# One joint order for the first two iterations of a two-block attention kernel, and identity products on TensorE ahead of it

## The chip, the cores and the metric

The kernel runs on one core of a Trainium2 chip. The metric is the device time of one execution in microseconds (us). All times come from three runs of the kernel before and one profiled execution of it.

## The reference, cut to what matters

Two residual attention blocks for 16 batch items `b`, all in float32. `x` is `(16, 256, 512)`.

```python
# block 0: 8 heads of 32, over 512 tokens, query = key = value
q = x^T @ Wq^T                       # per head qh
logits = (scale*qh@qh^T * cmask + (1-cmask)*-1e30) * rmask
x = x + (softmax(logits) @ qh @ Wo^T)^T
# block 1: 16 heads of 32, over 256 rows of width 512
xn = rms_norm(x, g_norm) * (1 + scale_b) + shift_b      # scale_b, shift_b = cond[b] @ W_emb + b_emb
q, k, v = split(xn @ W_qkv);  q, k = rms_norm(q, g_q), rms_norm(k, g_k)
o = softmax(q@k^T / sqrt(32)) @ v
x = x + o + o @ W_out
```

## The kernel before, in words

Work is written out by hand for each engine, and every engine follows its own list in order; semaphores join them. `pipeline(steady, special)` runs steps `i = -1 .. 17`. In step `i` block 0 of item `i` (stages A: heads 0 to 3, B: heads 4 to 7), block 1 of item `i-1` (stage C) and the output product of item `i-2` are interleaved. Steps 2 to 14 use one list, `iteration`; steps -1, 0, 15, 16 and 17 have lists of their own, and so the first two batch items meet only as far as those lists let them.

The steps, by the names used below:
- `project0` (L396): query projection, two float32 products of 128x512 into PX. ACT takes it (`take_query`, L1059), POOL masks it (`mask_query`, L1903), ACT rounds it to QHI and DVE makes the rest QLO (`split0`).
- `maxima0` (L411) and the DVE reduction L1539: row maxima of the raw scores, four key blocks for each of the two head groups. `rows0` (L426) transposes them; ACT sends them to row 96 of B0 with a DMA (L1079).
- `stack0`: six SP DMAs for each head, which put QHI and QLO under each other into A0 and B0. `score0` (L442) multiplies these; ACT takes the exponential (L1040) into a buffer of E. There are two score banks, PS0 and PS1.
- `values_weighted0` (L469), `weights_summed0` (L480; it needs the sums that `add_keys0` makes on POOL, L1916, and on DVE, L1557), `take_sums0` and `invert0` (DVE, L1577), `scale0`, `context0`, `out0` (L508), `residual0`, `squares`, `rstd`, `norm`, `norm_rows` (L519), `modulate`: from the probabilities of block 0 to XNT, the input of block 1.
- `qk` (L530), `take_heads`, `square_heads`, `square_sums`, `add_eps`, `power_heads` (POOL, L1928), `norm_heads` (POOL, L1935), `heads_rows` (L548), `round_heads`, `split1`, `maxima1` (L420, DVE L1546), `rows1` (L430), `stack1` (six SP DMAs for each of four), `values1`, `score1` (L456), `values_and_sums1` (L491, L494), `out1` (L564).
- `modulation` (L372): eight groups of four products of 128x128 by 128x16; a float32 product is two instructions on TensorE, so these are 64. They use WEMB, which before lies in E. ACT issues all weight loads (L1484 to L1492) before its first activation.

The order in which shared PSUM banks (PX, the four banks of PM, PO) pass from one user to the next is written in the tables BIG, MAXES and CONTEXT_TAKEN; `big`, `small` and `quad_free` turn them into waits. An instruction of TensorE that waits holds all that stands behind it in its list.

Of the kernel before, what the change touches and what calls it, by code (L numbers as in the profile page):

```python
# [7 lines left out]
F32 = mybir.dt.float32  # L8
F32R = mybir.dt.float32r
ALU = mybir.AluOpType  # L10
# [29 lines left out]
class Order:  # L40
# [4 lines left out]
    def __init__(self, *uses, special=None):  # L45
        self.uses, self.special = uses, special or {}

    def of(self, i):
        return self.special.get(i, self.uses)

    def find(self, key, i):
        return [k for k, _, _ in self.of(i)].index(key)

    def count(self, i, stop, place):
        return sum(0 <= i + off < NB and place in (None, where) for _, off, where in self.of(i)[:stop])

    def upto(self, key, i, place=None):

        if i < -1:
            return 0  # L60
        return sum(self.count(j, None, place) for j in range(-1, i)) + self.count(i, self.find(key, i) + 1, place)

    def ahead(self, key, i, place=None):

        return self.upto(key, i, place) - (place in (None, self.place(key)))

    def total(self, place):
        return sum(self.count(j, None, place) for j in range(-1, NB + 2))

    def place(self, key):  # L70
        return next(where for k, _, where in self.uses if k == key)
# [11 lines left out]
            (("C", 3), -2, 0), (("C", 0), -1, 0), (("C", 1), -1, 0), (("C", 2), -1, 0), ("A", 0, 0), ("B", 0, 0)),  # L83
        16: (
            ("A", 0, 0), ("B", 0, 0), (("C", 3), -2, 0), (("C", 0), -1, 0), (("C", 1), -1, 0), (("C", 2), -1, 0)),
# [32 lines left out]
            (("p1", 0), -1, 0), (("p1", 1), -1, 0), (("p1", 2), -1, 0), (("p1", 3), -1, 0), (("w1", 0), -2, 0),  # L118
            (("w1", 1), -2, 0), (("v1", 0), -1, 0), (("v1", 1), -1, 0), (("p0", 0), 1, 0), (("p0", 1), 1, 0),
            (("w0", 0), 0, 0)),  # L120
# [5 lines left out]
            (("p0", 0), 1, 0), (("p0", 1), 1, 0), (("w0", 0), 0, 0), (("p1", 0), -1, 0), (("p1", 1), -1, 0),  # L126
# [2068 lines left out]
```

## Time and profile before

| | us |
|---|---|
| median of 3 runs | 1313.63 |
| lowest, highest | 1311.67, 1318.56 |
| the profiled execution, its own time | 1316.98 |
| its span in the profile | 1315.2 |
| TensorE busy in the span | 1247.5 (95%) |
| VectorE, ScalarE, GpSimd busy | 1034.5, 767.3, 773.4 |
| mean granted TensorE clock, share of 2.4 GHz | 0.969 |

The span is what the engines show between first and last instruction; the time has 1.8 us more around it. TensorE is the busy engine, but its share is a mean over a long even middle and two ends that look different, so the views to read are those by stretch and the instructions in order of time at both ends.

### The profile page before, as it was taken

The numbers are of one execution on the slowest core, as the hardware profiler recorded it, in microseconds if no ns is written. First come the engines' busy times: TensorE is split into PE (matmuls) and PEld (weight loads), VectorE is DVE, ScalarE is ACT, GpSimd is POOL, SyncE is SP. The second block draws the span as 40 slices with busy tenths as digits, with TensorE's granted clock in tenths as the row PEclk, the third lists the DMA queues.
The fourth block names the chain that finished last, engine by engine and source line by source line (L and its number), as shares of the span: only waits on it lengthen the run. The fifth ranks groups of instructions, "written<-read, shape, count | busy, mean of one in ns | idle before, by whom it ended". The sixth has DMA issues, their size and how long they took to land.

```text
span 1315.2 us, 20714 instructions
## 1 busy us (share of the span) xinstructions
PE 1247.5 (95%) x6768; PEld 581.5 (44%) x6768; DVE 1034.5 (79%) x916; ACT 767.3 (58%) x1393; POOL 773.4 (59%) x391
## 2 busy tenths in 40 slices
PE   6979899999999999999999999999999999998877
PEld 4424354544444454444445454444545444443433
DVE  4665778878887887889787888888788888877654
ACT  1525566665656666565657666566666656564514
POOL 0245658476665838575574847566583766647442
PEclk8769899999999999999999999999999999999998
DMA  8322544437253433636354342735444363632332
GB/s 279 98 52 78 113 105 99 108 84 169 82 142 101 112 98 92 150 81 162 94 117 111 91 119 81 170 89 124 110 102 107 91 161 82 147 77 57 83 68 61
DMA packets 77960, 143.01 MB, mean 109 GB/s; under 512 B 21536, under 2 KB 23072, under 8 KB 77856
## 3 DMA queue, kind: packets, MB, share of 16 engines
q1 hardware_dynamic: 69136, 126.17, 39.1%
q10 hardware_dynamic: 8720, 15.51, 3.9%
q8 instruction: 58, 0.95, 0.3%
q14 instruction: 46, 0.38, 0.1%
HBM read 32.02 MB, written 8.39 MB: 31 GB/s over the span
## 4 chain that ended last, share of the span: by engine, by line
PE 80%; POOL 6%; issue 4%; DVE 3%; ACT 3%; SPq 2%; ACTq 1%; DMA 1%; POOLq 0%; DVEq 0%
PE PX L530 25%; PE PS L442 9%; PE PO L469 8%; PE PX L564 7%; PE PS L456 6%; PE PO L491 5%; POOL RQK L1928 5%; PE PM L411 4%; PE PX L508 2%; PE PM L508 2%; PE PO L494 2%; PE PM L420 2%; SPq L2071 1%; PE PM L480 1%; PE PM L548 1%
## 5 line engine op out<-in xcount | busy, mean ns | idle before, releaser
L1040 ACT ACTIVATE E<-PS,KBIAS 128x512 f32<-128x512 f32 x512 | 340.0, 686 | 199.0 <-PE PS L442 151.3
L530 PE MATMUL PX<-WQKV,XNT 128*128 128x512 f32 x768 | 383.9, 603 | 3.1 <-ACT V L1018 1.6
L1539 DVE TENSOR_REDUCE NM<-PM 128x4 f32<-128x2048 f32 x128 | 292.1, 2282 | 79.4 <-PE PM L411 79.4
L1916 POOL TENSOR_TENSOR E<-E 128x1024 f32<-128x1024 f32 x112 | 263.1, 2368 | 120.8 <-PE PO L469 107.6
L442 PE MATMUL PS<-B,A 97*128 97x512 f32 x512 | 288.1, 600 | 6.2 <-ACT E L1040 5.3
L1946 POOL TENSOR_TENSOR KQLO<-E 128x1024 f32<-128x1024 f32 x64 | 151.5, 2368 | 229.3 <-ACT E L1047 227.6
L1928 POOL TENSOR_TENSOR RQK<-RQK,HALF 128x16 f32<-128x16 f32 x64 | 211.1, 3303 | 96.6 <-DVE RQK L1627 96.6
L1047 ACT ACTIVATE E<-PS 128x512 f32<-128x512 f32 x256 | 146.9, 597 | 111.1 <-PE PS L456 110.9
L530 PEld LDWEIGHTS PX<-WQKV,XNT 128*128 128x128 f32 x768 | 136.5, 190 | 103.7 <-issue 89.1
L1546 DVE TENSOR_REDUCE NM<-PM 128x8 f32<-128x2048 f32 x64 | 146.4, 2288 | 37.5 <-PE PM L420 37.4
L442 PEld LDWEIGHTS PS<-B,A 97*128 97x128 f32 x512 | 93.3, 192 | 161.6 <-issue 110.2
L456 PE MATMUL PS<-B,A 97*128 97x256 f32 x512 | 136.6, 373 | 4.7 <-ACT E L1047 2.5
L469 PE MATMUL PO<-E,V 128*32 128x512 f32 x1024 | 139.4, 628 | 0.0
L564 PE MATMUL PX<-WOUT,OT 128*128 128x512 f32 x248 | 125.5, 600 | 0.9 <-ACT QK L1018 0.9
L1646 DVE RECIPROCAL T<-T 128x256 f32<-128x256 f32 x64 | 111.5, 1742 | 15.8 <-ACT T L1018 15.8
L456 PEld LDWEIGHTS PS<-B,A 97*128 97x128 f32 x512 | 81.3, 191 | 82.9 <-issue 64.3
L1557 DVE TENSOR_TENSOR E<-E 128x1024 f32<-128x1024 f32 x80 | 99.0, 1238 | 23.5 <-ACT E L1040 16.1
L1577 DVE RECIPROCAL R<-R 128x256 f32<-128x256 f32 x64 | 109.9, 1736 | 1.1
L1018 ACT ACTIVATE QK<-PX 128x512 f32<-128x512 f32 x64 | 38.2, 597 | 86.6 <-PE PX L530 86.6
L396 PE MATMUL PX<-XB,WQ 128*128 128x512 f32 x128 | 66.5, 645 | 10.5 <-DMA XB<-x 5.8
L411 PE MATMUL PM<-QHI 32*128 32x512 f32 x512 | 67.3, 514 | 8.5 <-DVE NM L1539 5.2
L1620 DVE TENSOR_REDUCE SSQ<-YSQ 128x16 f32<-128x512 f32 x64 | 43.7, 682 | 38.8 <-ACT YSQ L1103 37.6
(80 smaller groups left out, 1354.3 us busy)
## 6 DMA issues: line engine op xcount, KB each, us to landing
A<-QHI SPq DMA_DIRECT2D x256, 64.0 KB, 2.0
B<-QHI SPq DMA_DIRECT2D x256, 64.0 KB, 2.0
A<-KQHI SPq DMA_DIRECT2D x128, 128.0 KB, 2.4
B<-KQHI SPq DMA_DIRECT2D x128, 128.0 KB, 2.4
XB<-x SPq DMA_DIRECT2D x16, 512.0 KB, 4.0
A<-QLO SPq DMA_DIRECT2D x128, 64.0 KB, 2.0
B<-QLO SPq DMA_DIRECT2D x128, 64.0 KB, 2.0
X<-x ACTq DMA_DIRECT2D x16, 512.0 KB, 4.9
```

The lines of the kernel that those rows point to most:

```text
L442: mm(PS[n % 2][:, :], A0[0:97, h, g * P:(g + 1) * P], B0[0:97, h, :], start=True, stop=True).then_inc(score_full, 1)
L456: last = mm(PS[n % 2][:, kb * N1:(kb + 1) * N1], A1[0:97, hq, c, kb * P:(kb + 1) * P], B1[0:97, hq, c, :], start=True, stop=True)
L469: last = mm(PO[h * DH:(h + 1) * DH, :], V0[:, q, g, h * DH:(h + 1) * DH], E[:, probs(seg, i, g), h, :], start=(g == 0), stop=(g == KB0 - 1))
L530: last = mm(PX[:, :], XNT[:, c, t * P:(t + 1) * P], WQKV[:, c, part * DM:(part + 1) * DM], start=(c == 0), stop=(c == 3))
L564: last = mm(bank, OT[:, c, t * P:(t + 1) * P], WOUT[:, c, :], start=(c == 0), stop=(c == 3))
L1040: fn(E[:, probs(seg, i, g), h, :], PS[n % 2][:, :], ACT.Exp, bias=KBIAS[:, g, b:b + 1], scale=SCALE).then_inc(exp_done, 1)
L1047: fn(E[:, probs("C", i, c), h, :], PS[n % 2][:, :], ACT.Exp, scale=SCALE_RAW).then_inc(exp_done, 1)
L1539: v.tensor_reduce(NM0[:, q, :].rearrange("p (h k) -> p h k", k=KB0)[:, :, kb], PM[:, :, :], axis=AX.X, op=ALU.max, negate=True).then_inc(m ...
L1546: v.tensor_reduce(NM1[:, :].rearrange("p (h c a) -> p h c a", c=Q1, a=2)[:, :, c, :], PM[:, :, :].rearrange("p h (a k) -> p h a k", a=2), ...
L1916: g_.tensor_tensor(running(seg, i)[:, heads_, :], running(seg, i)[:, heads_, :], E[:, probs(seg, i, g), heads_, :], ALU.add).then_inc(done, 1)
L1928: g_.tensor_tensor(rqk, rqk, HALF[:, :], ALU.pow).then_inc(rqk_done.sem, 1)
L1946: g_.tensor_tensor(key_sums(c), e[:, :, 0:N1], e[:, :, N1:2 * N1], ALU.add).then_inc(esum_done.sem, 1)
```

## The change

It touches the first three and the last three lists, not `iteration`.

1. Steps 0 and 1 get one joint list, `iterations_0_and_1`, on every engine; step 1 is then empty. The tables get matching entries, and `Order` counts them with a dictionary instead of by walking.
2. `keep_warm(n)`: n products of the identity with itself into PS1, which nobody reads. The calls in the diff are 14, 4, 8, 8, 12, 8 and 16, 70 in all.
3. WEMB has its own place (over B1), is loaded by SP directly behind XB; WO, WQKV and WOUT are loaded by SP in `load_weights`, behind a wait for `row0_in[1]`. ACT issues only CT, BEMB, GN and GQK, at once.
4. ACT issues half of the first item's `stack0`.
5. `modulation` runs as two blocks of four groups, around the last `maxima0` of the first head group.
6. Step 15 gets another order (on POOL `masked_out` goes from the place behind the first `add_keys0` to the place behind the last `norm_heads`). In step 16 `qk` alternates between PX and a bank of PM, `norm_heads` is on DVE, `values_and_sums1` of item 14 goes behind the four `qk`, the rows of maxima go out in two halves (`rows1_half`, four DMAs each), and ACT issues one `stack1` of four. Step 17 has its `out1` in another order.

```diff
+            def keep_warm(n):
+                pe.wait_ge(ident_set.sem, 3)
+                for _ in range(n):
+                    mm(PS[1][:, 0:P], IDENT[:, :], IDENT[:, :], start=True, stop=True)
...
             def iteration_before(i):
+                keep_warm(14)
                 project0(i, i + 1, 0)
                 project0(i, i + 1, 1)
+                keep_warm(4)
                 maxima0(i, i + 1, 0, 0)
+                keep_warm(8)
                 maxima0(i, i + 1, 0, 1)
-                modulation(0)
-                modulation(1)
-                modulation(2)
+                keep_warm(8)
                 maxima0(i, i + 1, 0, 2)
-                modulation(3)
-                modulation(4)
-                modulation(5)
+                modulation(0, 1, 2, 3)
                 maxima0(i, i + 1, 0, 3)
-                modulation(6)
-                modulation(7)
+                modulation(4, 5, 6, 7)
                 rows0(i, i + 1, 0)
-
-            def iteration_0(i):
+                keep_warm(12)
+
+            def iterations_0_and_1(i):
+                maxima0(i, i, 1, 0)
+                keep_warm(8)
+                project0(i, i + 1, 0)
+                keep_warm(16)
+                score0("A", i, i, 0, 0, 0)
                 values0(i, i, 0)
...
                 score0("B", i, i, 1, 3, 0)
+                maxima0(i, i + 1, 0, 1)
+                project0(i, i + 1, 1)
+                maxima0(i, i + 1, 0, 2)
+                values_weighted0("B", i, 1, 1)
                 score0("B", i, i, 1, 3, 1)
...
                 weights_summed0("B", i, 1)
...
+                score0("A", i + 1, i + 1, 0, 0, 0)
+                values0(i + 1, i + 1, 0)
+                values0(i + 1, i + 1, 1)
+                score0("A", i + 1, i + 1, 0, 0, 1)
+                score0("A", i + 1, i + 1, 0, 0, 2)
+                score0("A", i + 1, i + 1, 0, 0, 3)
                 out0(i, i, 0)
                 out0(i, i, 1)
...
+                norm_rows(i, i)
+                score0("A", i + 1, i + 1, 0, 1, 2)
+                score0("A", i + 1, i + 1, 0, 1, 3)
+                qk(i + 1, 0, 0, 1, 2, 3)
...
             def iteration_16(i):
                 qk(i, 0, 0, 1, 2, 3)
-                values_and_sums1(i - 1, i - 2, 3)
                 qk(i, 1, 0, 1, 2, 3)
                 qk(i, 2, 0, 1, 2, 3)
                 qk(i, 3, 0, 1, 2, 3)
-                out1(i, i - 2, 0, 0, 1)
+                out1(i, i - 2, 0, 0)
+                values_and_sums1(i - 1, i - 2, 3)
...
+        def heads_bank(b, k):
+            return PM[:, 3, :] if b == NB - 1 and k % 2 else PX[:, :]
...
+            def load_weights():
+                sp.wait_ge(row0_in[1].sem, row0_in[1].at(0))
+                sp.dma_start(WO[:, :, :], wo_t.rearrange("(c p) n -> p c n", p=P)).then_inc(wo_in.sem, 16)
+                sp.dma_start(WQKV[:, :, :], w_qkv.rearrange("(c p) n -> p c n", p=P)).then_inc(wqkv_in.sem, 16)
+                sp.dma_start(WOUT[:, :, :], w_out.rearrange("(c p) n -> p c n", p=P)).then_inc(wout_in.sem, 16)
...
+            def iterations_0_and_1(i):
+                load_mask(i)
                 stack0(i + 1, 0, 2)
                 stack0(i + 1, 0, 1)
                 stack0(i + 1, 0, 3)
+                load_weights()
+                stack0(i + 1, 0, 0)
```

## Rows read from the trace of the kernel before

**Rows 1.** Busy time by stretch: length, PE, PEld, DVE, ACT, POOL, clock, DMA, GB/s.

```profile
200.00:275.50 75.50, 74.56 (x427) 34.78 (x419) 63.41 (x57) 47.72 (x88) 48.30 (x25) 1.00 0.46 113
1163.90:1243.10 79.20, 71.59 (x395) 32.87 (x395) 56.73 (x52) 45.50 (x81) 44.33 (x23) 0.98 0.32 77
1243.10:1286.40 43.30, 34.61 (x136) 14.57 (x133) 23.19 (x24) 9.50 (x16) 18.23 (x9) 0.96 0.32 71
1286.40:1315.20 28.80, 24.14 (x150) 12.14 (x148) 13.11 (x10) 12.29 (x22) 9.45 (x4) 0.87 0.13 42
104.00:182.00 78.00, 72.35 (x381) 32.83 (x381) 55.49 (x48) 47.03 (x86) 46.31 (x24) 0.92 0.37 86
37.40:103.90 66.50, 51.34 (x187) 19.18 (x187) 43.73 (x44) 28.42 (x51) 24.11 (x12) 0.71 0.31 79
```

**Rows 2.** Stretches of 2 us, TensorE alone: length, busy, clock, DMA, GB/s.

```profile
16.00:18.00 2.00, 2.00 (x7) 1.00 1.01 415
...
24.00:26.00 2.00, 2.00 (x11) 0.50 1.06 288
...
52.00:54.00 2.00, 1.93 (x12) 1.00 0.44 109
```

**Rows 3.** In order of time, the opening: start, length, engine, line, work, idle before.

```profile
12.14 1.28 ACT L1059 ACT_TABLE_LOAD   x1 [12.14 <-issue]
...
14.26 3.50 PE L396 MATMUL PX<-XB,WQ 128*128 128x512 f32 x4 [4.72 <-ACT QF L1059]
...
18.32 2.29 DVE L1539 TENSOR_REDUCE NM<-PM 128x4 f32<-128x2048 f32 x1 [1.40 <-PE PM L411]
...
27.29 5.30 PE L372 MATMUL PO<-CT,E 128*128 128x16 f32 x24
...
37.39 0.60 ACTq L1079 DMA_DIRECT2D B<-NMT  x1
...
37.46 1.09 PE L403 MATMUL PM<-IDENT,QF 128*128 128x128 f32 x4 [0.40 <-issue]
...
40.01 1.22 PE L442 MATMUL PS<-B,A 97*128 97x512 f32 x2
...
101.55 1.06 PE L519 MATMUL PM<-IDENT,YSQ 128*128 128x128 f32 x8 [0.16 <-DVE YSQ L1605]
```

**Rows 4.** In order of time, where the stages of steps 0 and 1 begin.

```profile
59.45 0.99 PE L442 MATMUL PS<-B,A 97*128 97x512 f32 x2 [0.41 <-DMA B<-NMT]
...
90.98 3.78 PE L508 MATMUL PX<-XB,WO 128*128 128x512 f32 x4 [0.58 <-DVE XB L1588]
...
103.89 1.95 PE L530 MATMUL PX<-WQKV,XNT 128*128 128x512 f32 x2
...
159.07 0.80 PE L456 MATMUL PS<-B,A 97*128 97x256 f32 x2
...
181.92 1.02 PE L530 MATMUL PX<-WQKV,XNT 128*128 128x512 f32 x2
```

**Rows 5.** Groups of the page: busy, mean ns of one, idle before and releaser.

```profile
L1916 POOL TENSOR_TENSOR E<-E 128x1024 f32<-128x1024 f32 x112 | 263.1, 2368 | 120.8 <-PE PO L469 107.6
...
L1577 DVE RECIPROCAL R<-R 128x256 f32<-128x256 f32 x64 | 109.9, 1736 | 1.1
```

**Rows 6.** DMA issues of the first 60 us: KB each, us to landing.

```profile
WQKV<-w_qkv ACTq DMA_DIRECT2D x1, 3072.0 KB, 15.2
...
WOUT<-w_out ACTq DMA_DIRECT2D x1, 1024.0 KB, 19.3
```

**Rows 7.** In order of time, the waits of steps 15 and 16.

```profile
1186.92 0.62 POOL L1907 TENSOR_SCALAR CBI<-CBI 128x512 f32<-128x512 f32 x1 [7.63 <-DMA CBI<-cond]
...
1195.35 1.94 PE L480 MATMUL PM<-E,ONES 128*32 128x512 f32 x8 [4.03 <-DVE E L1557]
...
1256.91 3.70 PE L530 MATMUL PX<-WQKV,XNT 128*128 128x512 f32 x8 [0.69 <-ACT QK L1018]
...
1267.11 1.09 PE L548 MATMUL PM<-IDENT,QK 128*128 128x128 f32 x8 [1.23 <-POOL QK L1935]
```

More of the change, by code:

```diff
@@ L324, in cond_resid @@
         n1_full = ev("n1_full", 1)
+        n1_half = [sem(f"n1_half{j}") for j in range(2)]
+        row1_half_in = [sem(f"row1_half_in{j}") for j in range(2)]
         row1_in = ev("row1_in", 16)
@@ L382, in small, with modulation @@
                 return PM[:, k, :]
+            def modulation(*ns):
+                pe.wait_ge(mod_in.sem, 16 * 3)
+                pe.wait_ge(ct_in.sem, 16)
+                for n in ns:
+                    for c in range(4):
+                        last = mm(PO[:, n * NB:(n + 1) * NB], WEMB[:, c, n * P:(n + 1) * P], CT[:, c, :],
+                                  start=(c == 0), stop=(c == 3))
+                if ns[-1] == 7:
+                    last.then_inc(mod_full.sem, 1)
+            def keep_warm(n):
+                pe.wait_ge(ident_set.sem, 3)
+                for _ in range(n):
+                    mm(PS[1][:, 0:P], IDENT[:, :], IDENT[:, :], start=True, stop=True)
             def quad_free(key, i):
@@ new lines, in iterations_0_and_1 @@
+                score1(i + 1, i, 1, 2)
+                score1(i + 1, i, 1, 3)
+                maxima0(i + 1, i + 2, 0, 2)
+                score1(i + 1, i, 2, 0)
+                out0(i + 1, i + 1, 0)
+                score1(i + 1, i, 2, 1)
+                score1(i + 1, i, 2, 2)
+                out0(i + 1, i + 1, 1)
+                score1(i + 1, i, 2, 3)
+                maxima0(i + 1, i + 2, 0, 3)
+                values_and_sums1(i + 1, i, 0)
+                score1(i + 1, i, 3, 0)
+                values_and_sums1(i + 1, i, 1)
@@ L873, in iteration_15 @@
-                score0("A", i, i, 0, 2, 3)
                 qk(i, 2, 3)
@@ L1047, in exp1, with stack0, stack1 @@
                 fn(E[:, probs("C", i, c), h, :], PS[n % 2][:, :], ACT.Exp, scale=SCALE_RAW).then_inc(exp_done, 1)
+            def stack0(b, q, hq):
+                act.wait_ge(qlo_done.sem, qlo_done.at(b, q + 1))
+                act.wait_ge(score_full, SCORES.upto(("AB"[q], 15), b - 1))
+                for dst, src in stack0_rows(q, hq):
+                    act.dma_start(dst, src).then_inc(stack0_in[q][hq].sem, 16)
+            def stack1(i, b, hq):
+                for k in range(4):
+                    bank = MAXES.place(("tq", k))
+                    act.wait_ge(bank_taken[bank], MAXES.upto(("tq", k), i, bank))
+                act.wait_ge(score_full, SCORES.upto(("C", 15), b))
+                for dst, src in stack1_rows(hq):
+                    act.dma_start(dst, src).then_inc(stack1_in[hq].sem, 16)
             def take_context0(seg, i, b, q):
```

808 lines of the change are left out of this document (544 added, 264 removed), and 12 rows, old and new, of the table special.

## The prediction

> **What bounds the kernel now.** I read the busy times by stretch first, because the change touches only the ends. In the even middle one step takes 75.5 us, of which TensorE is busy 74.6 at full clock [rows 1]: it is the bound there, and `iteration` is not changed, so steps 2 to 14 should give and take nothing. The front is another matter. Steps 0 and 1 take 66.5 and 78.0 us; TensorE is busy 51.3 and 72.4 of these, at a granted clock of 0.71 and 0.92 [rows 1], so part of the busy time is half-speed work. The end takes 79.2, 43.3 and 28.8 us with 71.6, 34.6 and 24.1 busy. There a chain over several engines is the bound, and TensorE waits in its places. So I then read the instructions in order of time at both ends, and ask for each stage which wait ends last.
>
> **The clock in the front.** Full clock at 16 to 18 us, behind four dense projection instructions; 0.50 at 24 to 26 although TensorE is busy the whole time with `modulation`; full again at 52 to 54, behind another projection [rows 2, 3]. So the dense wide products were followed by a rise, the modulation's narrow ones were not.
>
> **What one identity product costs.** It is two instructions with a 128x128 weight and 128 moving columns. The nearest rows are the transposes of the same shape: four in 1.09 us at low clock, eight in 1.06 at full [rows 3]. Taking off one latency (about 0.4 and 0.25 us) leaves 0.22 and 0.11 us each, so a product costs 0.44 us at the low clock and 0.22 at the high one. The ends are 0.27 and 0.13 an instruction with the latency spread in. All 70 cost 15 us high or 31 low.
>
> **The opening, step by step.** I take TensorE's start at 4.0 us, an estimate: it needs the WQ load, and not XB as the first projection did. Fourteen products end near 9.7 if the clock rises about two thirds through. Projection 1.7, to 11.4. ACT was held by its own DMA issues to 12.1 and then loaded its table in 1.28 [rows 3]; now five small issues end near 3.5 us, but the table load may still stand behind the wait (0 or 1.28; I take 1.28, since it sat in front of the activation). So `take_query` comes near 12.7, where it came at 13.4. With the second projection at full clock (1.7 for 3.5 [rows 3]) the first reduction starts near 16.8 for 18.3, gain 1.5. Each of the next rounds is bound by the 2.29 us reduction plus 0.7; eight products (1.8 high, 3.5 low) fit under that only at full clock. Modulation is 64 instructions, at 0.22 each 14.1 us at low clock, 7.0 at high [rows 3]. Full clock throughout would bring `rows0` to 30.3, where it was 36.7. But the modulation blocks are just what ran in the low stretch, so I expect the fall near 27 and `rows0` near 33.8. Its data lands about 2.6 us after the issue, as it did from 37.39 to 40.01 [rows 3], so near 37. What holds the first score is then TensorE's own list: 36 products, one `maxima0` and a projection. Twelve products low 5.3, maxima 0.6, eight high 1.8, projection 1.8, sixteen high 3.5: the first score at 46, **6 us later than before**. This is the price of the products that lie on the path; the first 34 are nearly covered. Ends: 40.5 (never low) and 51 (fall at once and products low to the sixteenth).
>
> The page on the clock of the Trainium skill (TensorE: Matmul & The Clock Gate, "What's actually happening") says that the chip sets the clock by how busy TensorE has been lately. Taken as share of busy time, that rule would keep the modulation at full clock and give the first score at 40.5; the row of 24 to 26 us, 2.00 busy of 2.00 at 0.50, speaks against it.
>
> **Stage A of item 0** took 59.45 - 40.01 = 19.4 us [rows 3, 4], with half of it at low clock. Now one maxima round and a projection are already done, and the clock is high. What ends last is three reductions in a row with one add between (3 x 2.3 + 3 x 0.6 + 1.2), a row transpose, a copy and the row's DMA, from 2 us after the first score: 15.
>
> **From stage B to the first `qk`**, before 103.89 - 59.45 = 44.4 [rows 4]. POOL is the long lane: first add 4.5 after the start, four adds of 2.37 [rows 5], a mask 1.3, `scale0` 1.3, one more add: sums ready at 21. On DVE `take_sums0` 0.7, two reciprocals of 1.74 [rows 5], scale and context 1.4: `out0` could start at 27.4. The maxima of item 1 go through DVE before this, 4 x 2.3, and fit between. In TensorE's list, though, four scores of item 1 stand ahead of `out0`, and the first needs a `stack0` that SP issues behind `load_weights`. These 4.25 MB took 15 to 19 us to land among other traffic [rows 6]; at the about 410 GB/s that the opening moved [rows 2] they need 10.5. SP is at them near 13.5; I take it that the stack waits for what its own queue holds ahead (if not, it lands in time and 3 us go), so it lands near 26, `out0` starts near 28.6. From `out0` to `qk` it took 12.9 [rows 4], with the first product block at low clock; at high, and with one reduction squeezed in, 10.9. Sum 39.5, gain 5.
>
> The Trainium skill (DMA: Bandwidth & Descriptors, "Queues, rings and completion order") says that one engine's ring is consumed in order. That agrees with the choice made here; no row of before shows it, since there the stacks and the weights had different issuers.
>
> **From the first `qk` to that of step 2**, before 78.0 [rows 1, 4]. Clock 0.92 means 12.5 us at half speed, costing 6.2; I let 5.5 of it go, since nothing thins TensorE's list there now. Eight scores, two transposes, one weighted value and one maxima of stage A are done beforehand: 6. Left: 66.5. The chain of item 0's heads does not forbid it: four `power_heads` and norms on POOL, four maxima, rows and stacks give 44 to the first C score, where it was 159.07 - 103.89 = 55.2 [rows 4], and the C stage keeps its 22.9.
>
> Front: 46 + 15 + 39.5 + 66.5 = 167.0 against 181.9 [rows 4], **gain 14.9**.
>
> **Step 15.** POOL stood 7.63 us before `masked_out` on the mask's DMA, with `power_heads` and `add_keys0` behind it; for this DVE's add came late and TensorE idled 4.03 us and ran the next 3 at half speed [rows 7]. Moving `masked_out` behind the heads takes this away: 5.5 us. Of the 7.6 idle in the step [rows 1] no more than 8 can go. Next late is the `stack1` chain, so I take 5.
>
> **Step 16.** `qk` on one bank ran 3.70 and a 0.69 wait [rows 7], four times; two banks drop three gaps of 0.85, and `values_and_sums1` goes behind them: 3.5. Heads now meet DVE's norm, not a POOL queue; I count it equal. Three stacks on SP instead of four, and halves of the rows: the last stack is 3.85 earlier, the first C score needs only the first half. Together 7 of the 43.3 us [rows 1]. The C stage after that gets eight ACT issues of half a microsecond and keeps its 28.8.
>
> End: **gain 12**, between 5 and 17.
>
> **The sum.** 1316.98 - 14.9 - 12 = 1290.1 for an execution like the profiled one. Its time lay 3.35 over the median, so 1313.63 - 26.9 = 1286.7, say 1287.
>
> **The rivals.**
> 1. *Clock high through the modulation.* First score at 40.5 and shorter products: 1281. For it: the products before and between. Against: rows 2. Chance 0.2.
> 2. *The joint list stalls.* The stack behind the weights lands not at 26 but with the 19.3 of WOUT added to 15.5, at 35, and `out0`, the scores and all of step 1 wait 9 us; another 4 are lost where `project0` now stands behind a maxima round and ACT's list behind `take_query`. 1300. For it: rows 6. Against: those loads shared the rings with more traffic. Chance 0.2.
> 3. *The products don't lift the clock, and lie on the path.* As modulation did, they keep TensorE busy at 0.50. Place: ahead of the first score. Then 14 + 4 + 16 products, both modulation blocks (14.1) and 36 more products (15.8) all run low, the first score is at 64, 18 later than in my sum; stage A takes 19.4 (+4.4) and B some 5 more; and if it also costs the clock of `qk`, 3 more: 1287 + 30 = 1317, slower than before. It decides from a first score at about 64: below that the end's 12 us cover it. Against: the transposes at 101.55 ran at full clock [rows 3], and a projection has the same weight. Chance 0.1.
> 4. My own case, 1279 to 1295: 0.5.
>
> **How the numbers follow.** 0.5 + 0.2 + 0.2 + 0.1. The likeliest gives 1287. The range reaches down past rival 1 with the end's better bound (1281 - 5, and the stack early, 3), to 1272, and up past rival 2 with a poor end (1300 + 5), 1305; rival 3 is outside. A measurement of this kernel can tell about 0.5%, 6.6 us, from no change. Faster by more (under 1307): 0.87, all but rival 3 and a thin part of rival 2. Within: 0.08. Slower: 0.05.
>
> **What would show it.** Right: granted clock 1.00 in the rounds of `maxima0`, a drop in the modulation, the first score near 46; `qk` of step 2 near 167; steps 2 to 14 at 75.5 each; the end from there 139 long in steps 15 to 17. Wrong: a first score before 42 or after 55; a score of item 1 waiting on a stack DMA for more than 5 us; a steady step that changed; POOL idle at `masked_out` without use to TensorE.

## The result, and the profile after

| | before | after |
|---|---|---|
| median, us (9 runs each, in turn) | 1316.17 | 1308.59 |
| lowest to highest | 1311.67 to 1318.56 | 1307.71 to 1313.58 |
| profiled execution, its span | 1316.98, 1315.2 | 1308.48, 1306.2 |
| mean granted clock | 0.969 | 0.982 |

The ratio is 0.9957 (0.9941 to 0.9973): the change takes 7.6 us off, where 27 were forecast, and 1287 lies 21.6 below what came. The signs were right, the size was not, and the time lies outside the range.

The first view is the stage borders, read from the instructions in order of time as in [rows 3, 4]. "First score" is item 0's first, "B" its first score of the second head group; times are in the span.

| start of, us | before | forecast | after |
|---|---|---|---|
| first score | 40.0 | 46 | 43.65 |
| stage B | 59.45 | 61 | 59.1 |
| `out0` of item 0 | 91.0 | 89.6 | 95.4 |
| first `qk` | 103.9 | 100.5 | 108.1 |
| C of item 0, its first score | 159.1 | 144.5 | 161.2 |
| `qk` of step 2 | 181.9 | 167.0 | 183.0 |
| from there to the end of the span | 1133.3 | 1121 | 1123.2 |

So the end gave 10.1 of the 12 forecast, and the front gave nothing: it is 1.1 longer. The rest of this text asks where its 16 us are.

The view by stretches of the kernel after (length, PE, PEld, DVE, ACT, POOL busy, clock, DMA share, GB/s). The rows are, in turn: to the first score; stage A; B to `out0`; `out0` to the first `qk`; to the first C score; to `qk` of step 2; an even step; steps 15, 16; the C stage at the end.

```profile
3.90:43.60 39.70, 37.89 (x236) 32.68 (x237) 19.65 (x22) 3.63 (x8) 3.15 (x3) 0.87 0.64 175
43.60:59.10 15.50, 13.25 (x65) 5.29 (x63) 8.72 (x5) 11.02 (x20) 6.03 (x3) 0.89 0.00 1
59.10:95.40 36.30, 24.46 (x106) 9.40 (x106) 23.76 (x18) 16.53 (x29) 14.12 (x7) 0.82 0.57 181
95.40:108.10 12.70, 9.89 (x33) 4.16 (x32) 5.83 (x8) 6.22 (x14) 3.09 (x2) 0.77 0.15 39
108.10:161.20 53.10, 48.02 (x213) 19.43 (x213) 36.97 (x34) 27.45 (x49) 34.37 (x18) 0.95 0.43 101
161.20:183.00 21.80, 19.30 (x151) 11.24 (x147) 17.84 (x19) 13.84 (x29) 7.80 (x4) 1.00 0.40 103
...
200.00:275.50 75.50, 74.58 (x420) 34.86 (x419) 63.48 (x57) 47.88 (x87) 48.38 (x25) 1.00 0.42 104
...
1165.60:1237.70 72.10, 69.47 (x393) 31.94 (x391) 52.44 (x50) 44.91 (x79) 45.97 (x22) 1.00 0.35 85
1237.70:1274.60 36.90, 32.51 (x134) 14.00 (x130) 26.77 (x30) 9.88 (x17) 14.28 (x5) 0.94 0.35 82
1274.60:1306.20 31.60, 24.97 (x153) 12.75 (x153) 9.85 (x10) 12.55 (x23) 9.46 (x4) 0.90 0.12 40
```

The even step is that of [rows 1], 75.5 with 74.6 busy. In B to `out0` TensorE is busy for 24.5 of 36.3: no other row above has as much idle time. TensorE in order of time, after, shows what it is:

```profile
91.06 0.80 PE L500 MATMUL PS<-B,A 97*128 97x512 f32 x1 [6.96 <-DMA B<-QLO]
...
95.42 3.61 PE L569 MATMUL PX<-XB,WO 128*128 128x512 f32 x4
98.83 2.31 PE L569 MATMUL PM<-XB,WO 128*128 128x512 f32 x4
...
105.72 1.21 PE L580 MATMUL PM<-IDENT,YSQ 128*128 128x128 f32 x8 [2.48 <-DVE YSQ L1882]
```

The first score of item 1 waits 6.96 us on a DMA of its stack. The context for `out0` was ready at 88.9, but its products stand behind that score. The queue of SP (second number: us spent on the issues) tells why the stack is late:

```profile
62.62 0.51 SPq L2439 DMA_DIRECT2D A<-QHI  x1
...
74.78 0.58 SPq L2427 DMA_DIRECT2D WO<-wo_t  x1
75.41 0.50 SPq L2428 DMA_DIRECT2D WQKV<-w_qkv  x1
75.95 0.51 SPq L2429 DMA_DIRECT2D WOUT<-w_out  x1
76.56 0.51 SPq L2439 DMA_DIRECT2D A<-QHI  x1
...
79.65 0.59 SPq L2439 DMA_DIRECT2D B<-QLO  x1
```

Three other stacks are issued from 62.62 on, the weights behind them at 74.78, and this head's stack at 76.56 to 80.24. It lands near 91, 11 us after its last issue. Windows of 2 us (length, PE, PEld, DVE, ACT, POOL, clock, DMA share, GB/s) show the DMA engines full up to 88 and at 0.82 behind it, and the clock going down at the end of the wait:

```profile
80.00:82.00 2.00, 1.04 (x9) 0.24 (x9) 2.00 (x3) 0.63 (x2) 0.61 (x1) 1.00 1.00 421
...
84.00:86.00 2.00, 0.10 (x4) 0.00 (x0) 1.97 (x2) 1.11 (x2) 0.00 (x0) 1.00 1.00 383
...
88.00:90.00 2.00, 0.00 (x0) 0.00 (x0) 0.87 (x2) 0.00 (x0) 0.00 (x0) 0.86 0.82 238
```

So `out0` ran at the low clock (3.61 us for four instructions; 1.97 in e5 below). The first `qk` block did too, 6.27 us for eight, but behind another wait: the 2.48 us on DVE at 105.72. Between the two the clock was up again, since eight instructions took 1.06 us at 101.31.

### The profile page after: what moved, and what is told of

It is laid out like the page before. It is cut to its first block, busy times and chain, and to the rows that moved or that the text cites. A ratio compares the mean times of both kernels' runs of the same rounds, so it can differ in the third digit from the quotient of the medians.

```text
span 1306.2 us, 21009 instructions
## 1 busy us (share of the span) xinstructions
PE 1249.7 (96%) x6909; PEld 594.1 (45%) x6909; DVE 1030.0 (79%) x920; ACT 768.3 (59%) x1394; POOL 767.7 (59%) x387
## 4 chain that ended last, share of the span: by engine, by line
PE 74%; POOL 6%; DVE 6%; SPq 5%; issue 4%; ACT 2%; DMA 2%; ACTq 1%; DVEq 0%
PE PX L598 24%; PE PS L500 8%; PE PO L530 7%; PE PX L632 6%; PE PS L517 5%; POOL RQK L2266 5%; PE PO L552 5%; SPq L2447 4%; PE PM L463 4%; PE PX L569 2%; PE PM L569 2%; PE PO L555 2%; PE PM L472 2%; PE PM L580 1%; PE PS L434 1%
## 5 line engine op out<-in xcount | busy, mean ns | idle before, releaser
L598 PE MATMUL PX<-WQKV,XNT 128*128 128x512 f32 x752 | 377.6, 606 | 0.7 <-DVE XNT L1889 0.3
L2254 POOL TENSOR_TENSOR E<-E 128x1024 f32<-128x1024 f32 x112 | 262.9, 2366 | 118.0 <-PE PO L530 95.4
L500 PE MATMUL PS<-B,A 97*128 97x512 f32 x512 | 285.3, 593 | 12.7 <-DMA B<-QLO 7.0
L2266 POOL TENSOR_TENSOR RQK<-RQK,HALF 128x16 f32<-128x16 f32 x64 | 211.4, 3310 | 81.0 <-DVE RQK L1904 80.6
L598 PEld LDWEIGHTS PX<-WQKV,XNT 128*128 128x128 f32 x752 | 134.7, 192 | 101.0 <-issue 91.5
L530 PE MATMUL PO<-E,V 128*32 128x512 f32 x1024 | 134.5, 607 | 0.6 <-ACT E L1207 0.6
L517 PEld LDWEIGHTS PS<-B,A 97*128 97x128 f32 x512 | 81.6, 191 | 84.8 <-issue 67.7
L552 PE MATMUL PO<-E,V 128*32 128x256 f32 x1024 | 68.5, 385 | 0.3 <-ACT T L1185 0.3
```

The lines of the kernel that those rows point to most:

```text
L500: mm(PS[n % 2][:, :], A0[0:97, h, g * P:(g + 1) * P], B0[0:97, h, :], start=True, stop=True).then_inc(score_full, 1)
L517: last = mm(PS[n % 2][:, kb * N1:(kb + 1) * N1], A1[0:97, hq, c, kb * P:(kb + 1) * P], B1[0:97, hq, c, :], start=True, stop=True)
L530: last = mm(PO[h * DH:(h + 1) * DH, :], V0[:, q, g, h * DH:(h + 1) * DH], E[:, probs(seg, i, g), h, :], start=(g == 0), stop=(g == KB0 - 1))
L598: last = mm(bank, XNT[:, c, t * P:(t + 1) * P], WQKV[:, c, part * DM:(part + 1) * DM], start=(c == 0), stop=(c == 3))
L2254: g_.tensor_tensor(running(seg, i)[:, heads_, :], running(seg, i)[:, heads_, :], E[:, probs(seg, i, g), heads_, :], ALU.add).then_inc(done, 1)
L2266: g_.tensor_tensor(rqk, rqk, HALF[:, :], ALU.pow).then_inc(rqk_done.sem, 1)
```

## The experiments

Kernels of one table were timed in turns with the kernel before, whose medians were 1314.8, 1314.2, 1314.6, 1315.2 and 1313.6 in the five sets of runs (the last set is e17 and e18). "Base" is the kernel of e5, and of e9. Medians and ratios with intervals:

| run | us | ratio to before | first score | first `qk` | `qk` of step 2 |
|---|---|---|---|---|---|
| e1 stack ahead | 1305.4 | 0.9937 (0.992 to 0.9955) | 44.0 | 103.9 | 178.0 |
| e2 end only | 1307.9 | 0.9949 (0.9936 to 0.9962) | 39.9 | 103.8 | 181.8 |
| e3 no products | 1303.6 | 0.9925 (0.9909 to 0.994) | 38.5 | 105.3 | 179.4 |
| e4 34 early products | 1299.1 | 0.9891 (0.9874 to 0.9908) | 35.9 | 104.3 | 179.2 |
| e5 early, stack ahead | 1296.3 | 0.9865 (0.9846 to 0.9883) | 36.0 | 91.8 | 167.1 |
| e9 the same again | 1299.2 | 0.9867 (0.9843 to 0.9891) | 39.0 | 98.5 | 172.6 |
| e6 none, stack ahead | 1295.8 | 0.9861 (0.9849 to 0.9874) | 37.6 | 98.0 | 171.7 |
| e17 the same again | 1298.8 | 0.9881 (0.9858 to 0.9905) | 37.9 | 98.7 | 172.6 |
| e7 early, early weights | 1301.0 | 0.99 (0.9886 to 0.9914) | 39.5 | 100.2 | 175.5 |
| e8 early, separate lists | 1307.2 | 0.9953 (0.994 to 0.9966) | 38.4 | 101.8 | 179.2 |
| e10 short reciprocals | 1298.9 | 0.9868 (0.9845 to 0.9892) | 36.1 | 100.8 | 175.5 |
| e11 maxima first | 1298.2 | 0.9871 (0.9849 to 0.9894) | 36.1 | 96.1 | 173.7 |
| e12 half rows by SP | 1295.9 | 0.9862 (0.9836 to 0.9888) | 36.4 | 96.7 | 171.5 |
| e13 norm first | 1301.6 | 0.989 (0.9863 to 0.9917) | 39.0 | 99.3 | 174.4 |
| e14 short values | 1298.5 | 0.9869 (0.9852 to 0.9886) | 36.1 | 100.5 | 175.7 |
| e15 early mask | 1306.2 | 0.9923 (0.9906 to 0.9941) | 36.1 | 98.7 | 173.9 |
| e16 none, norm first | 1300.0 | 0.9884 (0.9864 to 0.9904) | 37.8 | 102.3 | 175.9 |
| e18 none, half rows by SP | 1300.7 | 0.9895 (0.9873 to 0.9918) | 37.6 | 98.4 | 173.8 |

The last three columns come from one profiled execution, the median from four to six; where both are read, note that e4's profile was its slowest execution (1304.2) and e5's its fastest (1292.2). Medians of different sets are compared below too. Where their intervals overlap, the difference is not shown, and the text says so.

### Two suspects: the stack's place and the late products

e1, the stack issued ahead of the weights:

```diff
-                load_weights()
                 stack0(i + 1, 0, 0)
+                load_weights()
```

> One line moved in SP's joint list: the stack of head 0 of item 1 is issued ahead of the three weight loads, not behind them. In the trace after, the first score of item 1 waited 6.96 us for that stack (it landed at 91, issued 76.6 to 80.2, behind 4.25 MB issued from 74.8), with the out0 products behind it although their input was ready at 88.9. Theory A (the stack waits in SP's own ring behind the weights, and TensorE's list hangs on it): the score goes near 84.5, out0 near 89.5 where it was 95.4, the whole run 5 to 7 us shorter than the changed kernel, near 1302. Theory B (the DVE chain to the context is what ends last anyway, or the DMA engines are the limit, so that the stack is as late): within 1 us of the changed kernel, 1308.

The wait on the stack is gone from the trace, `out0` starts at 91.5 for 95.4, and the median falls by 3.2. That is less than theory A had, and as the two intervals overlap it is not clear of the scatter. A wait of 2.6 us with no releaser named is left at the same score. The DMA view of 78 to 83 us (KB of each, us from issue to landing) tells what it is, first after, then e1:

```profile
B<-QLO SPq DMA_DIRECT2D x1, 64.0 KB, 11.4
B<-NMT ACTq DMA_DIRECT2D x1, 8.0 KB, 4.9
```

```profile
B<-QLO SPq DMA_DIRECT2D x1, 64.0 KB, 2.1
B<-NMT ACTq DMA_DIRECT2D x1, 8.0 KB, 5.1
```

The stack's transfers, ahead of the weights, land in 2 us for 11. The row of maxima that the same score needs, 8 KB on ACT's queue, still takes 5.1 us beside the weights; in the opening of before it took 1.8. It was issued at 81.99, so it landed at 87.1, and the score starts at 87.17. The same sum gives the start of that score within 0.2 us in e5, e6, e9 and e12, where the row took 4.9 to 6.3. So the weights hold this score in two ways, and the earlier stack takes away one.

e2 has the front of before and the end of after:

> Steps -1, 0 and 1 and the weight loads as in the kernel before, with no products; steps 15 to 17 as in the changed kernel. Theory A (the end carries all of the gain, the front gives nothing or takes a little, as the stage starts of the two traces say: the end 10.3 us shorter, the front 1.1 longer): 10 us under the kernel before, 1306, that is 1 to 3 under the changed kernel. Theory B (the end's gain depends on the state in which the front leaves the pipeline, or the front gives its part): 1310 or more.

It takes 7.0 us off the kernel before: no difference is shown to the 7.6 that the whole change gives.

e3 leaves all products out, e4 the 36 behind the last `rows0` of the opening:

```diff
-                keep_warm(12)
...
-                keep_warm(8)
                 project0(i, i + 1, 0)
-                keep_warm(16)
```

> The changed kernel without the 70 identity products, all else the same. Theory A (products on the path cost more than the clock gives: 36 of them stand ahead of the first score): the first score near 36 to 39, stage A at the low clock some 4 us longer, the end 2 to 4 us earlier, 1305. Theory B (they hold the clock up, and without them the opening runs at 1.2 GHz all through): first score no earlier than 40, stage A 19 us as before, stage B starts later than 59; 1312. Theory C (what decides the front is the stack behind the weights, and any gain ahead of it is swallowed there): 1308 within 1.

> The changed kernel with the first 34 products and without the 36 between the row transpose and the first score. Theory A: first score near 36, 7.5 earlier; stage A longer by 3 at low clock; stage B 4 us earlier, and 3 to 4 of that is kept: 1304.5. Theory C (the weights and the stack behind them start earlier too, since SP's stacks of item 1 hang on round_query in stage A): as much. Theory B (without them the clock stays low to 52 as before): 1309 or more.

Without any the kernel is 5 us faster than with all, about as theory A had it; without the 36 late ones 9.5, where theory A had 4. In the trace of after these 36 take 4.21, 2.05 and 3.73 us, 10 in all, ahead of the first score with nothing beside them. They do bring stage A at a higher clock, 15.4 us for 19.3 in e4 (each from the first score to the seventeenth, which is B's first), but the first score is 7.8 later, so B starts 3.9 later. Both then wait 7 us for the same stack, and the clock is lost in that wait.

e5 and e6 put the stack ahead in e4 and e3:

> The 34 products of the opening kept, the 36 ahead of and behind project0(1,0) left out, and the stack of head 0 of item 1 issued ahead of the three weight loads. With all 70 products the earlier stack alone gave 3.2 us (1308.6 to 1305.4), without the 36 late ones 9.5 (to 1299.1). Theory 1 (two separate costs: the late products take TensorE's time ahead of the scores, and the stack behind 11 us of weights idles it 7 us and then drops its clock): the two add, 1296, first qk block at 99 to 101 in the span, no DMA wait above 1 us at a score of item 1. Theory 2 (one slack: whichever is removed, the next wait, DVE's sums of squares for the norm, takes its place): 1299, qk at 103 to 104, and the wait on DVE ahead of it grows to over 4 us.

> No products at all, and the stack of head 0 of item 1 issued ahead of the weight loads. Beside the run without products (1303.6), with early ones (1299.1) and with all (1308.6) it completes a table of products by place of the stack. Theory 1 (the stack's wait is a cost of its own): 1300 to 1301, the DMA wait of 5.8 us gone, qk near 101. Theory 2 (the next wait takes its place): 1303 to 1304. The early products, against none, are worth 4.5 us with the stack behind; theory 1 expects 3 to 5 with the stack ahead too.

Medians by products (down) and place of the stack (across):

| | behind the weights | ahead |
|---|---|---|
| all 70 | 1308.6 | 1305.4 |
| 34 early | 1299.1 | 1296.3, 1299.2 |
| none | 1303.6 | 1295.8, 1298.8 |

Both suspects are real, and they are different ones. The late products cost 6 to 9.5 us with the stack at either place, with intervals that lie apart. The stack's place costs 5 to 8 us without any products, again with intervals apart. With all products it is 3, and beside the early ones 0 to 3, and there the intervals overlap. The early products show no worth once the stack is ahead: 11 runs with them have a median of 1297.2, 10 without (e6, e17) 1297.5. Two later pairs point opposite ways, e13 and e16 by 1.6 us for leaving them out, e12 and e18 by 4.8 for keeping them, both with intervals that overlap, so a few us either way stay open.

> The kernel with no products and the stack ahead of the weights a second time (1295.8, four runs from 1295.2 to 1297.6). Theory 1 (the early products buy nothing in the mean; the scatter between 1292 and 1301 is that of the clock in the front): 1295 to 1299, as with the products. Theory 2 (with them the kernel is better by the 1.6 to 4.5 us of the first score and of the other pair of runs, and the first run without them was a good one): 1299 or more.

e7 tried the other cure: the weights load in the opening, directly behind WEMB, and the stack stays where it is.

> The 34 products of the opening kept, the 36 late ones left out; the three weight loads issued right behind the small weights of the modulation in the opening, without the wait for the row constants, where nothing else is on SP's queue; the stack stays at its place in the list, with no weights ahead of it. Theory 1 (the weights, not the stack's place, are the cost): no DMA wait at a score of item 1, 1295 to 1297, and the first score no later than 36.5. Rival (the weights delay what the opening needs, the embeddings' loads and item 0's first stacks): first score over 38 and the time at or above 1299.

The DMA wait went here too, and the row of that head landed in 1.8 us with no weights beside it. But the first score came at 39.5 for 35.9, as the rival had it, and 1301.0 is 2 to 5 behind e5 and e9: the same 4.25 MB now stand ahead of the data of the opening. The start at 39.5 alone would not show it, since e9 has 39.0 by its clock. The trace does: TensorE waited 1.26 us for the second item's XB, and the first score's row took 6.9 us to land, where e9 has 2.6 and no such wait.

### What the joint list gives

e8 keeps the opening with 34 products and takes steps 0 and 1 as the separate lists of before:

> The opening of the changed kernel with its 34 early products, but steps 0 and 1 as the separate lists of the kernel before (weights behind the fourth stack of step 0), and the end of the changed kernel. Against the run with only the changed end (1307.9) it differs by the opening alone, against the run with the joint list and the same early products (1299.1) by the joint list alone. Theory 1 (the joint list is worth some 6 us through work taken ahead and fewer idle stretches, the opening 3): 1304 to 1306. Theory 2 (the opening's earlier first score and its higher clock is the whole gain): 1299 to 1300, with the first qk at 100 or below.

1307.2 beside e2's 1307.9: the opening alone gives nothing, and the joint list, e4 against e8, 8.1 us. Where they come from is shown in part only, since the two profiled executions took the same time (1304.0 of e8, its fastest, and 1304.2 of e4). Of what they show, 2 to 4 lie behind the first `qk`: from there to `qk` of step 2 the old lists took 78.0 (before), 78.0 (e2) and 77.4 (e8), the joint one 73.6 to 75.4 in sixteen profiles of seventeen (e11 is the other).

### Why that stretch is 75 and not 66.5

The stretch is the one from the first `qk` to the `qk` of step 2. In the trace of after the chain of waits runs over DVE from 146 to 168: the maxima of item 0's heads, with reciprocals of item 1 between them.

```profile
149.04 2.29 DVE NM L1823
151.33 1.66 DVE R L1854
152.99 2.15 DVE NM L1823
155.13 1.32 DVE R L1854
156.70 1.60 DVE NM L1816
```

e10 takes the reciprocals away (8 of 256 columns), e11 only changes the order:

```diff
-                r0 = R0[:, half * (T0 // 2):(half + 1) * (T0 // 2)]
+                r0 = R0[:, half * (T0 // 2):half * (T0 // 2) + (8 if b == 1 else T0 // 2)]
```

> On that base, the four reciprocals of item 1's sums work on 8 columns of 256 instead of all (part of the computation is left out: item 1's sums are not inverted). Four DVE instructions of 1.74 us go from the stretch between the first qk and that of step 2, which took 75.3 here where I had forecast 66.5, and in which the chain of waits runs over DVE from 146 to 168 in the changed kernel. Theory 1 (DVE is the bound there, and work taken ahead on TensorE frees nothing): the stretch falls by 4 to 6, to 69 to 71, and the time to 1290 to 1292. Theory 2 (TensorE is the bound): the stretch falls by at most 1, to 74 or more.

> On that base, in DVE's list of step 1 the first reciprocal of item 1's sums goes behind the fourth maximum of item 0's heads instead of ahead of it. The same work in another order. If DVE's list is the bound, the first C score comes 1.7 earlier (53.5 behind the first qk to 51.8), and the context of item 1, which then waits for both reciprocals as before, keeps its time, so that the stretch to step 2 loses 0 to 1.7. If it is not, neither moves.

The four reciprocals of e10, by shape (busy, mean ns):

```profile
L1851 DVE RECIPROCAL R<-R 128x8 f32<-128x8 f32 x4 | 0.7, 184 | 0.0
```

6.2 us of DVE's time are gone, and the stretch takes 74.8, at most 0.5 less. Theory 1 falls: an engine that carries the chain by the trace is not yet the bound. In e11 the first C score came no earlier (53.95 behind the first `qk`, 53.45 in e5) and the stretch grew to 77.6, because TensorE then waited 2.42 us for a sum of keys that DVE adds behind the reciprocals.

e14 takes three quarters of the value products of item 1 from TensorE:

> On that base, the 32 value products of item 1 in step 1 work on 128 of 512 columns (part of the computation is left out: the rest of item 1's weighted values). The page's group of these products has some 0.125 us for each at full clock; in the stretch from the first qk block to that of step 2 there are 56 to 64 instructions, 7 us of TensorE's time, of which three quarters go. Theory 1 (TensorE's own work is the bound in that stretch): it falls from 75 by 4 to 5. Theory 2 (a chain over the maxima on DVE, the rows and their DMA is the bound): by at most 1.5, with TensorE's idle time larger by the rest.

The stretch took 75.2, unchanged. But this run doesn't tell what it was made for. Windows of 2 us in it (columns as above):

```profile
134.00:136.00 2.00, 2.00 (x12) 1.02 (x12) 1.93 (x1) 1.76 (x4) 0.74 (x1) 0.68 0.73 158
136.00:138.00 2.00, 2.00 (x11) 0.71 (x10) 0.44 (x2) 0.69 (x1) 2.00 (x2) 0.50 0.94 205
138.00:140.00 2.00, 2.00 (x4) 0.95 (x4) 2.00 (x1) 1.26 (x2) 2.00 (x2) 0.50 0.91 199
```

TensorE got the low clock here, where e10 had 1.00, and its busy time in the stretch fell only from 67.7 to 66.7 (e5 to e14). What was taken away came back as slower work. The window ahead of the fall differs from the matching one of e10 in TensorE's busy time, 1.18 us of 2 beside 1.82 (e14, then e10):

```profile
132.00:134.00 2.00, 1.18 (x18) 0.65 (x10) 0.75 (x1) 2.00 (x6) 0.00 (x0) 1.00 0.00 0
134.00:136.00 2.00, 1.82 (x18) 0.70 (x10) 0.77 (x2) 2.00 (x6) 0.00 (x0) 1.00 0.00 0
```

That the shorter products are the reason is likely, but it is one profile each.

What does move the stretch is the clock at its start. The eight instructions of the first `qk` block took between 4.9 and 6.7 us, where full clock gives 3.60, and the stretch goes with them: 5.11 and 73.8 (e6), 5.41 and 74.1 (e9), 6.11 and 74.8 (e12), 6.64 and 75.3 (e5). What lies behind the block is 68.7 us long in thirteen of the seventeen profiles, to within 0.1. The others are e10 (68.3, so its reciprocals were worth 0.4), e14 (69.8), e13 (70.2) and e11 (72.1). With a block of 3.60 the stretch would be about 72.3, an estimate from these rows, and still not 66.5. So e13 tried to take the wait ahead of it (2.48 us for the norm, in front of which DVE has a maximum of 2.29):

```diff
-                maxima0(i + 1, i + 1, 1, 0)
                 norm(i, i)
+                maxima0(i + 1, i + 1, 1, 0)
```

> Base is again the kernel with 34 early products and the stack ahead of the weights (1296 to 1299). In DVE's list of step 0, item 0's norm goes ahead of the maximum of 2.29 us that stands in front of it. TensorE waits 2.5 us for that norm ahead of the transposes in front of the first qk block, and its clock is at 0.50 when the block runs (6.6 for 8 instructions, at full clock 3.6). Theory 1 (the wait and the clock it takes are a cost of their own): from out0 to the first qk falls from 10.5 to about 9, the wait on DVE below 1.5, the block to 3.6 to 5, time 1.5 to 4 us less. Theory 2 (the norm then waits on POOL's power instead, and the maximum comes late for the next round): no more than 0.5 less.

```profile
96.16 1.94 PE L580 MATMUL PM<-IDENT,YSQ 128*128 128x128 f32 x8 [3.44 <-DVE NM L1813]
```

The wait grew to 3.44, on the maximum itself: by that releaser the transposes need a PSUM bank that this maximum still reads. Neither theory had that, and 1301.6 is no gain: it lies 2.4 above e9, with intervals that overlap. e16, the same without products, has the same wait of 3.4 us and lies within 2 us of e13, as its theory 1 had it:

> No products at all, the stack ahead of the weights, and the norm ahead of the maximum. Without the last it took 1295.8, beside 1296.3 and 1299.2 with the 34 early products. Theory 1 (the products of the opening buy an earlier first score, 36.0 against 37.6, and nothing after it): this runs as the kernel with early products and the norm first, within 2 us. Theory 2 (they keep the clock through stage A, which took 14.3 in the best profile with them and 19 without): this is 3 to 5 us slower than that kernel.

### The end

e15 puts `masked_out` and the adds in front of the norms back into their old order in step 15:

> On that base, in step 15 POOL's masked_out goes back to its place of the kernel before, ahead of the second power of the heads, with the adds in front of the norms as there. Theory 1 (its 7.6 us wait on POOL's queue made the adds late, and TensorE waited 4.0 for the sums): step 15 grows from 72.1 by 3 to 5, with the wait for E of 4 us back. Theory 2 (with the second order of TensorE's list in step 15 the adds have slack): by less than 1.

Step 15 took 80.6 us for 72.1, more than theory 1 had: TensorE idles 7.49 us on POOL's norm of the heads.

```profile
1190.97 1.12 PE L616 MATMUL PM<-IDENT,QK 128*128 128x128 f32 x4 [7.49 <-POOL QK L2270]
```

POOL stood 3.96 us on the mask's DMA there, with the powers and norms of the heads behind it. That wait of TensorE is not the one on E of theory 1. In the new order of TensorE's list the place of the mask, with the add beside it, is worth 8.5 us, the largest piece found; what each of the two is worth wasn't taken apart.

The last stage is 2.8 longer after (31.6 for 28.8). e12 moves the four issues of the second half of the rows from ACT to SP:

```diff
 ACT  rows1_half, j == 1:
-                for h in range(QH):
-                    act.dma_start(B1[96:97, h, 2 * j:2 * j + 2, :]..., NMT1[h * QH:(h + 1) * QH, j, :]...)
 SP   iteration_16:
                 stack1(i, i - 1, 2)
+                rows1_half(i, i - 1, 1)
```

> On that base, the four DMA issues of the second half of item 15's rows go from ACT's list to SP's, behind its third stack. In the changed kernel those four took 2.42 us on ACT between two exponentials, and the stretch from the first C score of item 15 to the end grew from 28.8 to 31.6. Theory 1 (ACT's issues delay the exponentials, and TensorE stands behind them): that stretch falls by 1.5 to 2.5, to 29 to 30. Theory 2 (the second half lands late whatever issues it, TensorE waits for the DMA, and the clock falls): it changes by less than 0.7.

The stretch fell from 32.7 (e5, e9) to 32.1. That is under theory 2's limit of 0.7, but it shows nothing of theory 2's cause: the other profiles with the changed end have this stretch at 30.7 to 32.7 without the edit, so 0.6 is scatter. What it spends is in TensorE's list at its start (after):

```profile
1274.60 1.19 PE L517 MATMUL PS<-B,A 97*128 97x256 f32 x4 [1.55 <-issue]
1276.99 0.80 PE L517 MATMUL PS<-B,A 97*128 97x256 f32 x2 [1.20 <-DMA B<-KQLO]
1278.71 1.42 PE L517 MATMUL PS<-B,A 97*128 97x256 f32 x2
```

The first scores start earlier than the data of the second stack, wait 1.20 for it, and run at the low clock. Before, products of `values1` lay between them. So the gain of a first C score that comes early is in part given back here. This is read from the two traces; no run changed that order.

> No products, the stack ahead of the weights, and the second half of item 15's rows issued by SP. With the products that last edit measured 1295.9 beside 1299.2, of which the profiles showed 0.6 in its own stretch (32.7 to 32.1). Theory 1 (worth what its stretch shows): within 1 us of the kernel without it. Theory 2 (3 us): 1293.

1300.7 beside e17's 1298.8 in the same set, with intervals that overlap, and the stretch is 31.5 for 31.3: no gain, and theory 2 falls.

### The scatter

> The kernel with 34 early products and the stack of item 1 ahead of the weights once more (1296.3, runs from 1292.2 to 1301.1), as the base of the next three and for a second profile. Step 2 to the end took 1122.3 to 1123.3 us in the profiles of all nine kernels with the changed end, so the scatter must come from the front. Theory: a profile with a longer time has its first qk later than 91.8 or the stretch from it to step 2 longer than 75.3, at a lower clock; the end is unchanged. Rival: the steady steps scatter, 75.5 each by over 0.1.

From `qk` of step 2 to the end the profiles with the changed end took 1121.5 to 1124.8 us (e15 aside), so 3 us at most come from there; the first `qk` of one and the same kernel came at 91.8 and at 98.5. Of the 7.3 us between the spans of e5 and e9, 5.5 lie ahead of step 2 and 1.8 behind it: the theory has the larger part, and of the rest the steady steps take 1.5, 0.12 each, which is the rival's. Windows of TensorE alone (length, busy, clock, DMA, GB/s), first e5, then e9:

```profile
22.00:24.00 2.00, 2.00 (x20) 1.00 1.11 235
24.00:26.00 2.00, 2.00 (x19) 1.00 1.06 235
26.00:28.00 2.00, 2.00 (x12) 0.52 1.03 232
36.00:38.00 2.00, 1.75 (x9) 0.92 0.63 202
```

```profile
22.00:24.00 2.00, 2.00 (x18) 0.87 1.06 199
24.00:26.00 2.00, 2.00 (x12) 0.50 1.10 239
26.00:28.00 2.00, 2.00 (x11) 0.50 1.04 227
36.00:38.00 2.00, 2.00 (x6) 0.50 0.65 162
```

The clock falls inside the modulation, in e9 some 2.5 us earlier; it is back only behind 40, where e5 had it at 36, and the first score is 3 us later. The two fastest of these 11 runs (1292.2, 1292.9) had a mean clock of 0.986 and 0.985, the two slowest (1300.7, 1301.1) 0.979.

## Why the prediction was wrong, point by point

- **Even steps, the view of the whole:** right. 75.5 each, nothing moved.
- **The opening:** the mechanism was right. Clock 1.00 in the rounds of `maxima0`, 0.65 at 24 to 26 and 0.50 behind it (the fall was forecast near 27), `rows0` at 31.8 (33.8 forecast), first score at 43.65 for 46. A product took 0.26 us at the high clock (eight in 2.05) and 0.35 where the clock was low for part of them (twelve in 4.21), where I had 0.22 and 0.44. The 36 late ones took 10.0 for 10.6. Rival 1 didn't come, nor rival 3: the products lift the clock; modulation doesn't hold it. The trace again has TensorE busy 2.00 of 2.00 at 0.50 there.
- **Stage A:** 15.4 for 15.
- **B to the first `qk`: the first step that failed,** 49.0 for 39.5. The parts: the stack landed 32 behind B and not 26, since SP came to the weights at 15.7 and not 13.5, needed 5.5 us for the issues of the weights and the stack, for which I had left 2, and the queue ran at 238 to 311 GB/s in the last 4 us, not 410. I had named "waits on a stack DMA for more than 5 us" as the sign of a wrong forecast. To this come 4.4 us for scores and transposes at low clock between that landing and `out0`, where I had 2.6, and 12.7 for 10.9 to the `qk`. That was rival 2's mechanism at two thirds of its size (6 us late, not 9). With the stack ahead the stage takes 40.7 to 41.6 us where `out0` ran at full clock (e5, e6, e9, e11, e17, e18) and 44.3 to 45.7 where it didn't (e1, e10, e12 to e16). So the place of `load_weights` on one queue was the main term, and a smaller one was missing in the lane over POOL and DVE. POOL was ready at 21.5 behind B, for 21. Behind it stand an add of 1.22 us on DVE and TensorE's sums, which the forecast left out, so `take_sums0` came at 24.2 and the context at 29.8, for 27.4. That shows only where the stack is early. The stack's transfers land in 2 us when they are issued first (e1) and in 11 behind the weights. The rule of the Trainium skill on rings (DMA: Bandwidth & Descriptors, "Queues, rings and completion order"), which I had cited, agrees with that.
- **First `qk` to step 2: the second step that failed,** 74.9 for 66.5. I took 5.5 for the clock and 6 for work done ahead. TensorE's busy time fell from 72.4 to 67.3, which is both together, and its idle time rose from 5.6 to 7.6. Two sizes were wrong. The low clock went only in part: 0.95 over 53.1 us is 5.3 at half speed, where it was 12.5, so about 3.6 of the 5.5 came. The rest sits in the first `qk` block, behind the DVE wait (6.27 us for 3.60). What lies behind that block fell from 72.6 to 68.7; these 3.9 us are all that the clock there and the work done ahead gave together, where I had 6 for the work alone. And the chain of the heads, which I had at 44 us to the first C score, takes 53 in every run with the joint list (51.8 to 54.0), whether 6 us of DVE's work are gone (53.05) or TensorE's products are shorter (53.35). The C stage behind it, 21.9 for 22.9, starts only when that chain ends, so the work taken ahead on TensorE had little to shorten. Which of its links would have to go is not settled: the one run that took TensorE's work away was overlaid by the clock.
- **Front as a whole:** forecast -14.9, came +1.1.
- **Step 15:** 6.7 for 5. Putting the mask and one add back costs 8.5 (e15), though by a wait on the norm of the heads, not by the 4.03 us on E that I had read. **Step 16:** 6.4 for 7; `qk` on two banks ran 3.60 a block without a gap. **C stage:** -2.8 for 0. By the trace the scores start ahead of their second stack; no run tested that. Sum 10.3 for 12.
- **The bridge to the median:** I took 3.35 off since the profile lay over the median of three runs. Nine runs have it at 1316.17, so 2.5 of the 21.6 us are this; the front is 16.0 of them, the end 1.9. The last 1.2 are around the span (2.3 us for 1.8) and in the changed kernel's profile, which lay at its median where that of before lay 0.8 above its own.
- **Sums that don't close:** `rows0` at 33.8 and the 13.0 us behind it make 46.8, not 46. The terms named for POOL make 19.0, not 21, and those for DVE bring 21 to 26.6, not 27.4. The low end of the range is 1273 by its terms, not 1272. None of these is near the 16 us.
- **Chances:** rival 2 had 0.2 with 1300. It was the right rival, but I let it act alone: none of my cases held a stretch behind the `qk` that gains only 3, so the range stopped at 1305.

The best kernels here, e5 and e6 with their repeats e9 and e17 (the joint list, the stack ahead of the weights, at most the 34 early products), are at 0.9861 to 0.9881 of the kernel before, some 17 us, and some 11 below the changed kernel.

## What to carry to other kernels

When a list is joined across two iterations, ask of every load which small transfer stands behind it on the same queue, and count the issues too. Ask it of other queues as well: the 8 KB row came on another queue and still took 5 us beside the weights. Work taken ahead counts only if the other chain of the same stretch gets shorter as well; so size that chain from its own rows before the sum is made. And products that only hold the clock cost their full time if nothing else bounds that place: here 10 us of them put the first score 7.8 later and bought 3.9 in the next stage.

## What the runs showed of the hardware that I had not expected

- Modulation's products (128x16) went from clock 1.00 to 0.50 with TensorE busy 2.00 of 2.00, 2.5 us earlier or later in one and the same kernel. With value products cut from 512 to 128 columns (e14) the clock fell to 0.50 too, behind a window with TensorE busy 1.18 of 2 us, where the whole ones had 1.82 and kept 1.00: taking work away can cost the clock. That is one profile each.
- The identity products at the very start (28 instructions in 5.09 us, 0.18 each) ended at full clock, and the projection behind them ran at full speed, 1.88 us for four instructions beside 3.50 [rows 3]. The clock column shows 1.00 at both places, so in the first 18 us the lengths of the instructions tell the clock and the column doesn't.
- The transfers of one stack, behind 4.25 MB on one queue, landed 11 us after their last issue, with the DMA engines full; issued first they took 2. A row of 8 KB on the other queue took 4.9 to 6.3 us beside the same weights, and 1.8 without them (e7).
- One kernel's executions spread over 8.8 us (1292.2 to 1301.1); its two profiles have the first `qk` 6.7 us apart, and the steady part 1.5 (981.6 and 983.2 from `qk` of step 2 to that of step 15).
